# Post-norm attention and butterfly layer on one core: products with V in two visits a unit instead of three, probability ring of ten slots

## What is computed

```python
q, k, v = x @ w_q, x @ w_k, x @ w_v             # 16 heads of 64
p = softmax(q k^T / sqrt(64) + causal mask)     # 1024 x 1024 a head
x = layernorm(x + (p @ v) @ w_o)
h = gelu(butterfly(x @ W_exp + b_exp) + up_bias)      # 512 hidden, 9 butterfly stages
x = layernorm(x + butterfly(h) @ W_con + b_con + down_bias)
```

## Time and profile before

| what | value |
|---|---|
| median of 3 executions | 1036.18 us (1035.88 to 1036.36) |
| the profiled execution's own time | 1035.9 us |
| span, first to last instruction of it | 1034.2 us |
| mean granted TensorE clock | 0.993 of full speed |
| PE busy | 1007.0 us, 97% of the span |
| DVE busy | 778.0 us, 75% |
| POOL busy | 750.9 us, 73% |
| ACT busy | 613.1 us, 59% |

### The profile page before, as it was taken

The page is one execution under the profiler, slowest core; times in us unless marked ns, Lnnn a source line. Parts: engine busy times, 40 slices in busy tenths (PEclk is TensorE's granted clock), DMA queues, the critical chain, the costliest instruction groups (busy, mean ns, idle before and its releaser), DMA issues.

```text
span 1034.2 us, 17742 instructions
## 1 busy us (share of the span) xinstructions
PE 1007.0 (97%) x5816; PEld 697.7 (67%) x5816; DVE 778.0 (75%) x2112; ACT 613.1 (59%) x1246; POOL 750.9 (73%) x715
## 2 busy tenths in 40 slices
PE   6799999999999999999999999999999999999997
PEld 4566676676666776676666766767666766765687
DVE  7767777877777777878788778877778888785356
ACT  3555656566656656666556656666555656665544
POOL 6567887777768887777778877777778887777510
PEclk8899999999999999999999999999999999999999
DMA  6233122233222222232232222332222222320002
GB/s 190 62 83 82 45 72 53 62 83 83 58 68 62 63 65 60 63 83 63 70 76 58 62 56 55 83 83 63 66 60 74 63 57 57 83 64 22 22 11 73
DMA packets 48602, 68.71 MB, mean 66 GB/s; under 512 B 15191, under 2 KB 25083, under 8 KB 48510
## 3 DMA queue, kind: packets, MB, share of 16 engines
q1 hardware_dynamic: 48510, 67.57, 25.3%
HBM read 31.11 MB, written 2.36 MB: 32 GB/s over the span
## 4 chain that ended last, share of the span: by engine, by line
PE 92%; DVE 3%; DMA 2%; ACT 1%; issue 1%; POOL 0%; SPq 0%; POOLq 0%; ACTq 0%
PE O L717 25%; PE WORK L631 14%; PE SC L692 14%; PE SC L696 13%; PE WORK L644 6%; PE WORK L679 3%; PE WORK L607 3%; PE WORK L609 3%; PE WORK L608 3%; PE WORK L772 2%; PE WORK L617 1%; PE WORK L619 1%; PE WORK L618 1%; DVE WORK L991 1%; DMA R<-RROW 1%
## 5 line engine op out<-in xcount | busy, mean ns | idle before, releaser
L863 ACT ACTIVATE PR<-SC 128x512 f32<-128x512 f32 (+3 forms) x768 | 352.3, 490 | 263.9 <-PE SC L696 231.4
L519 POOL TENSOR_TENSOR SUM<-SUM,PR 128x1024 f32<-128x1024 f32 (+3 forms) x256 | 419.0, 1637 | 14.8 <-POOL SUM L528 0.5
L991 DVE CUSTOM_DVE_ANT_0 WORK<-WORK,CMASK 128x128 f32<-128x128 f32 (+3 forms) x512 | 239.3, 514 | 65.7 <-PE WORK L631 65.6
L692 PE MATMUL SC<-QH,KHL 128*128 128x512 f32 (+3 forms) x768 | 268.8, 356 | 3.1 <-ACT PR L863 3.0
L696 PE MATMUL SC<-QL,KH 128*128 128x512 f32 (+3 forms) x768 | 261.7, 346 | 3.3 <-DMA QL<-NROW 3.3
L504 POOL TENSOR_SCALAR_AFFINE_SELECT PR<-PR 128x256 f32<-128x256 f32 x256 | 105.9, 415 | 198.0 <-ACT PR L863 197.9
L631 PE MATMUL WORK<-KHL,QH 128*128 128x512 f32 (+3 forms) x768 | 226.5, 365 | 5.9 <-DMA KH<-KHL 4.1
L717 PE MATMUL O<-PR,VLO 128*64 128x512 f32 (+3 forms) x1024 | 200.0, 522 | 0.3 <-DVE OT L1075 0.3
L692 PEld LDWEIGHTS SC<-QH,KHL 128*128 128x128 f32 x768 | 145.2, 189 | 60.7 <-ACT PR L863 28.5
L631 PEld LDWEIGHTS WORK<-KHL,QH 128*128 128x128 f32 x768 | 136.7, 191 | 59.3 <-issue 35.4
L994 DVE TENSOR_REDUCE MP<-WORK 128x1 f32<-128x512 f32 x256 | 164.1, 684 | 4.8
(11 more groups left out here) (132 smaller groups left out, 1099.0 us busy)
## 6 DMA issues: line engine op xcount, KB each, us to landing
QH<-QH SPq DMA_DIRECT2D x128, 128.0 KB, 2.4
KH<-KHL SPq DMA_DIRECT2D x128, 128.0 KB, 2.3
R<-RROW SPq DMA_DIRECT2D x64, 256.0 KB, 3.8
SW<-in_L_ffn_up_weights_dram SPq DMA_DIRECT2D x9, 512.0 KB, 4.4
SW<-_L_ffn_down_weights_dram SPq DMA_DIRECT2D x9, 512.0 KB, 4.3
out_dram<-X SPq DMA_DIRECT2D x7, 256.0 KB, 2.3
X<-in_L_attn_x_BSE_dram SPq DMA_DIRECT2D x3, 512.0 KB, 4.5
X<-in_L_attn_x_BSE_dram SPq DMA_DIRECT2D x2, 256.0 KB, 3.3
```

The costliest lines, as they stand in the source:

```text
L519: nc.gpsimd.tensor_tensor(total, total, prob(unit, s), ALU.add).then_inc(add_done, 1)
L692: nc.tensor.matmul(dst, KHL[:, par, h, kt * P:(kt + 1) * P], QH[:, par, h, q0:q0 + n], start=True, stop=False)
L863: nc.scalar.activation(prob(unit, s)[:, h, :], SC[use % NSC][:, 0:n], ACT.Exp, scale=K ** -0.5).then_inc(exp_done, 1)
L991: op = nc.vector.tensor_tensor_reduce(cols, cols, CMASK[:, CH - n:], 1.0, LOWEST, ALU.add, ALU.max, cell)
```

## The change

Steps 0 to 6 are multiplied with V in one visit behind step 9, so a unit has visits of five and seven steps; `FILL` stays as it is. The ring PR has ten slots. The room for it comes from VLO, which has three slots (all even units share slot 0, odd ones take 1 and 2 in turn), and from R0, which becomes the first half of R. With that, ACT's copy of V waits for the products of the unit before (and not of the pair before), its copy of the row sums waits for the scaling two units back, BLOCKS moves into W1, and SP waits for the bias row to have landed before it loads W_exp, with the load of X put ahead of that wait.

```diff
-PRING = 9
+PRING = 10
...
-PV_AFTER = {1: [-5, -4, -3, -2, -1], 8: [0, 1, 2, 3], 9: [4, 5, 6]}
+PV_AFTER = {1: [-5, -4, -3, -2, -1], 9: [0, 1, 2, 3, 4, 5, 6]}
...
-        VLO = sb("VLO", [P, 4, TPC, 2 * K])
+        VLO = sb("VLO", [P, 3, TPC, 2 * K])
...
-        R0 = sb("R0", [P, CH])
         R = sb("R", [P, CHUNKS, CH])
...
-        BLOCKS = R[0:HT, 0, 0:P]
+        BLOCKS = W1[0:HT, 0:P]
...
+        R0 = R[:, 0, :]
         BROW = R0[0:1, :]
...
         def v_units(u):
 
-            return (u + 1, 4, 0) if u % 2 else (u, 2, TPC)
+            return (u + 1, 0) if u % 2 else (u, TPC)
+
+        def low_slot(u):
+
+            return (1 + u // 2 % 2) * (u % 2)
 
         def values(u, kt):
 
-            return VLO[:, u % 4, kt, :] if kt < TPC else VHI[:, u % 2, kt - TPC, :]
+            return VLO[:, low_slot(u), kt, :] if kt < TPC else VHI[:, u % 2, kt - TPC, :]
...
             sp.wait_ge(blocks_done, 1)
             sp.dma_start(BROW, BLOCKS).then_inc(brow_in, 16)
+            sp.dma_start(X[:, TILES:2 * TILES, :], x_tiles[:, TILES:2 * TILES, :]).then_inc(in_x[2], 16)
+            sp.wait_ge(brow_in, 16)
             sp.dma_start(W1[:, :], W_exp).then_inc(in_exp, 16)
-            sp.dma_start(X[:, TILES:2 * TILES, :], x_tiles[:, TILES:2 * TILES, :]).then_inc(in_x[2], 16)
             rows(0)
...
                 elif f[0] == "v":
-                    unit, slots, tile = v_units(u)
+                    unit, tile = v_units(u)
                     if f[1] == 0 and u > 0:
 
-                        act.wait_ge(pv_done, (u - u % 2) * NS + PV_CREDIT)
-                    V = VHI if tile else VLO
-                    dst = V[:, unit % slots:unit % slots + 2, 2 * f[1]:2 * f[1] + 2, :].rearrange("p u t k -> p t u k")
+                        act.wait_ge(pv_done, u * NS + PV_CREDIT)
+                    pair = VHI if tile else VLO[:, 0:low_slot(unit + 1) + 1:low_slot(unit + 1), :, :]
+                    dst = pair[:, :, 2 * f[1]:2 * f[1] + 2, :].rearrange("p u t k -> p t u k")
                     hi(dst, w[:, :].rearrange("p (t u k) -> p t u k", t=2, u=2)).then_inc(free, 1)
...
                     act.wait_ge(sums_landed, (u - 1) * 16 + 16)
+                    act.wait_ge(o_free, (u - 1) * CHUNKS + O_CREDIT)
                     nc.scalar.activation(R0[:, :], w[:, :], ACT.Copy).then_inc(sums_out, 1)
```

More of the change, by code:

```diff
@@ L610, in filler @@
                 elif f[0] == "v":
-                    unit, _, tile = v_units(u)
+                    unit, tile = v_units(u)
                     if f[1] == 0:
```

## The result

The changed kernel takes 1073.91 us (median of 4 runs, 1073.38 to 1078.33) against 1036.03 us: ratio 1.0376, 95% interval 1.0355 to 1.0396. The forecast was 1070 us. Two executions of some 3457 us, one of the kernel before and one of experiment 1's kernel, are unexplained and count in no ratio. The profiled execution has a span of 1071.7 us, 37.5 us more than before. Lines of the changed kernel are five or six higher than before: its L636 is L631 of the rows ahead of the prediction, L697 and L701 the scores, L722 the products with V, L1081 the scaling, L997 and L1000 the maxima, L869 the exponentials. In the kernels of experiments 3 to 6 that read fewer columns, DVE's lines are two higher again where they are made from the changed kernel (L999, L1002, L1083).

The account below looks back on a forecast made before the run. PE bounds the kernel (97% busy, 92% of the chain), other engines only where PE waits. 1035.9 us plus 33.8 us (26.7 + 2.2 + 5.5 - 0.6) gives 1069.7, given as 1070 us; range 1058 to 1085 us.

Parts of the forecast that it names:

- The gain: one visit fewer: PE's products with V: dropping one visit a unit saves 0.36 us, 11.5 us over 32 units; the seven-step visit lasts 4.88 us.
- The new wait: PE at max products 15 to 20 waits 1.25 us for WORK banks DVE reads late; unit 0.89 us longer, saving included.
- Over the units: Sum over the kernel: 26.7 us for units 1 to 30, +2.2, +5.5 and -0.6, together 33.8 us longer.
- The scaling's waits for the inverses: DVE's 11 waits before scaling, 5.5 us together, delay product 11 one for one and now reach PE: +5.5 us.
- The transposition's term: In 11 units the transposition takes one more bank behind product 16: 0.2 us each, 2.2 us.
- rival B: Each unit's row of waits also drops PE's clock, losing 1.7 us a unit: 1121 us; 5 in 100.
- The last unit: Unit 31 has no maxima, so it only saves; with the first unit -0.6 us.
- unit 0: The first unit scales nothing, so it only saves; with unit 31 -0.6 us.
- The rest of the change: Tenth slot, copies on ACT and the altered start: 0 us taken; the slot might give 0 to -3 us.
- SP's wait: At the start SP waits for the bias row before W_exp; some 8.8 us hide it: 0, at worst under 1 us.
- A: At product 16's bank: DVE is no bound and the saved visit stays saved, 1024.4 us; 8 in 100.
- C: DVE catches up for part of the gap, so mean wait equals the 0.36 us saved: 1036 us; 2 in 100.

Follow-up runs that it names:

- experiment 1: The changed kernel with the three visits of before (steps 0 to 3 behind step 8, 4 to 6 behind step 9): 1035.42 us, ratio 0.9998.
- experiments 3 to 6: In order: changed kernel, maxima 13-14 over 128 columns, 1052.29 us; maxima 11-16, 1044.52; kernel before, maxima 11-16, 1034.42; changed kernel, maxima 11-16 plus SCALE_AFTER = 8, 1023.22.
- experiment 6: The changed kernel with SCALE_AFTER = 8 and DVE's reads of products 11 to 16 over 128 columns only: 1023.22 us, ratio 0.9879.
- Experiments 2 and 3: The changed kernel, first with SCALE_AFTER 6 -> 8: 1031.01 us; then instead with DVE's maxima of products 13 and 14 over 128 of 512 columns: 1052.29 us.
- experiment 2: The changed kernel with DVE scaling the unit before behind step 8's maxima, not step 6's (SCALE_AFTER 6 -> 8): 1031.01 us, ratio 0.9955.

## Why the prediction was right

**The gain: one visit fewer.** Right: 0.36 us forecast, 0.33 measured a unit in experiment 6, and the seven-step visit lasts the 4.88 us forecast.

**The new wait.** Right, and to 0.01 us in the unit that was worked out: 0.89 us longer forecast, 29.94 - 29.05 = 0.89 measured. PE started 0.05 us behind the reader's end (0.06 in the earlier trace rows), and from DVE's end of 16 at 236.76 these 0.05, then 0.24, 0.10 and 0.09 us lead to the visit at 237.24, as in the forecast's sum. Experiments 2 and 3 show that it is DVE's row that PE follows, its start as much as its length.

**Over the units.** The sum came out 33.8 us where the span shows 37.5, and that the two are so near is in part luck, since errors of both signs are in it. From the first five-step visit to the start of the last unit's interval, units 1 to 30, the changed kernel took 38.0 us more, where 34.4 were forecast. The scaling's waits for the inverses were 8.0 us where I had carried 5.5 over from before (60 to 985 us of the changed kernel):

```profile
DVE OT L1081 <- DMA R<-RROW: 8.0, 14, 1.1
```

The transposition's term, forecast at 0.2 us a unit, was nearer 0.1 in the units without such a wait, 1.1 us less over the eleven. The clock added 1.1 us, since rival B happened once. In the window view of the changed kernel, and PE's start on product 15 in that unit:

```profile
293.00:296.60 3.60, 2.23 (x10) 1.16 (x9) 3.13 (x9) 1.34 (x3) 3.46 (x3) 1.00 0.00 0
296.60:300.00 3.40, 3.40 (x10) 2.10 (x11) 3.37 (x11) 1.37 (x3) 3.40 (x4) 0.50 0.00 0
...
295.21 0.83 PE L636 MATMUL WORK<-KHL,QH 128*128 128x384 f32 x2 [1.27 <-DVE MP L997]
```

This is one of the units in which the inverses were latest (DVE waited 1.03 us). PE stood idle for 1.27 us and in pieces after it, 2.23 us busy of 3.60, and then the clock was 0.50, 1.2 GHz, for 3.40 us. The unit took 32.5 us, against 31.4 for another that also has a transposition, in which DVE waited 1.06 us; taken against the same units before, the low clock cost some 1.1 us. In that other unit and in one more PE stood idle even a little longer, and the clock stayed at 1.00:

```profile
539.82 0.82 PE L636 MATMUL WORK<-KHL,QH 128*128 128x384 f32 x2 [1.30 <-DVE MP L997]
...
723.69 0.82 PE L636 MATMUL WORK<-KHL,QH 128*128 128x384 f32 x2 [1.32 <-DVE MP L997]
```

So the length of the idle time alone does not decide, and what does was not found. The Trainium skill, page "TensorE: Matmul & The Clock Gate", section "A second HAM failure mode: psum-queue depth-cycling", tells of a kernel whose short idle times, frequent enough, made the clock go to and fro. In this execution all of the 30 units had such waits, and the clock fell in one of them: 1.1 us in all, not the 51 of rival B. Why the one run at 1078.33 us was slower than its three neighbours, and whether by more such stretches (its mean clock was 0.987 against 0.989 to 0.991), was not traced and stays open.

With +2.5, -1.1 and +1.1 us the 34.4 become 36.9, which leaves 1.1 us of the 38.0; about half of that is one unit in which DVE was late for another landing (it waited 0.85 us for the row sums at its reciprocal). The last unit cost 0.8 us and not -0.3: ACT had no time to catch up, a wait that I looked for only in units with other work between the scores. Ahead of the first five-step visit and behind the last, 0.6 and 0.7 us went away where the forecast had 0.3 for unit 0 and nothing else; experiment 1's kernel, which merges nothing, has 0.7 and 0.8 us less there too, so these are not the visit's. Together 38.0 + 0.8 - 0.6 - 0.7 = 37.5 us.

**The rest of the change.** Right at 0 (experiment 1). At the start SP's wait was hidden, as forecast.

**Rivals.** A fell in the change as made, but its price was right. Another place for the scaling alone gives 4.7 us of it (experiment 2), and with shorter reads besides it gives all 11.2 (experiment 6). B happened in one unit of 30. C has nothing for it.

## What to carry to other kernels

Before a visit, a drain or a pause is removed from the bounding engine, look at what the other engines do in it. Here a visit cost TensorE some 0.35 us of overhead a unit, and while it lasted, VectorE had 2.3 us to empty four banks; with the visit gone from there, the banks decided. Start from the instruction that frees the first bank, count the consumer's work up to the bank that the last producer needs, and if that is later than the producer comes, move the consumer's other work (here a scaling whose result is wanted only later) behind it: the merging pays only together with that, -0.5% instead of +3.8%. And a busy share close to 100% does not say that nothing waits: where records overlap, as TensorE's do here, short waits are counted as busy (21.6 of 37.5 us), and only the distance between starts, the chain or the waits of the weight loads show them.

## What the runs showed that was not expected

- TensorE's clock fell once inside the attention, which it never did before: 1.27 us idle, with further short waits behind it, and then 3.40 us at 1.2 GHz. Idle times of 1.30 and 1.32 us in two other units of the same execution left it at 2.4 GHz.
- Reading six products over a third of their columns, in about half the time (1.49 us and not 3.05), left 21 us of waits that one moved instruction pair removed: 1044.5 us against 1023.2. The first wait of a row is not a matter of the row's rate but of its start.
- A plain maximum over 128 columns costs 282 ns and one over 512 columns 684 ns on DVE, so a quarter of the columns is 41% of the time.
